# Routed experts: the inner rows are turned by a transposing DMA instead of by TensorE

## The reference, cut to what matters

```
h   = (x @ W1[e]) * silu(x @ W3[e])        # 256 -> 512 inner features
y   = h @ W2[e]                            # 512 -> 256
out = sum over the two experts of gate * y
```

## Time and profile before

| | us |
|---|---|
| median of 3 runs | 1129.15 (1126.81 to 1134.13) |
| the profiled execution, its own time | 1125.32 |
| its span | 1123.5 |
| mean granted TensorE clock, share of full speed | 0.967 |
| PE busy over the span | 1001.6 (89%) |
| POOL busy over the span | 568.2 (51%) |

### The profile page before, as it was taken

How to read it: one execution, slowest core, us unless ns; L and a number is a source line. 1 busy time by engine, 2 the same in 40 slices (tenths; PEclk the granted TensorE clock), 3 DMA queues, 4 the chain that set the end, 5 groups by cost and what they waited for, 6 DMA issues and landing times. The chain is left out here.

```text
span 1123.5 us, 27288 instructions
## 1 busy us (share of the span) xinstructions
PE 1001.6 (89%) x9398; PEld 770.3 (69%) x9398; DVE 745.6 (66%) x1732; ACT 547.1 (49%) x1091; POOL 568.2 (51%) x743
## 2 busy tenths in 40 slices
PE   5898888677699899999999999949998995999998
PEld 3666666455488756666666666627787884898987
DVE  6999999756376634444544445558999974666663
ACT  5888888632255433333332222334443434766764
POOL 6776767205354479999991293047656501000000
PEclk9999999978699999999999999979999998999999
DMA  4454444347599684554221111323443312111110
GB/s 140 149 160 150 143 152 130 98 143 223 184 310 323 216 247 154 170 174 160 86 62 48 48 53 53 99 80 104 127 131 114 109 38 66 39 58 38 56 48 29
DMA packets 113819, 137.96 MB, mean 123 GB/s; under 512 B 12352, under 2 KB 102432, under 8 KB 111904
## 3 DMA queue, kind: packets, MB, share of 16 engines
q1 hardware_dynamic: 104464, 101.63, 29.0%
q0 software_dynamic: 9232, 34.67, 9.3%
HBM read 83.96 MB, written 52.30 MB: 121 GB/s over the span
## 5 line engine op out<-in xcount | busy, mean ns | idle before, releaser
L1121 ACT CAST hT<-HT 128x512 f16<-128x512 f32 x71 | 41.7, 587 | 184.5 <-PE HT L1063 184.5
L943 POOL DMA_INDIRECT xs_d<-ht,slot x64 | 67.2, 1050 | 85.8 <-DMA ht<-h_d 39.3
L1070 PE MATMUL Ye<-wm,hT 128*128 x852 | 105.1, 273 | 1.7 <-DVE hT L1155 1.5
L1070 PE MATMUL Ge<-wm,xT 128*128 x426 | 104.8, 383 | 1.0 <-DVE xT L1159 1.0
L1070 PE MATMUL Ue<-wm,xT 128*128 x426 | 103.7, 379 | 0.0
L1070 PEld LDWEIGHTS Ye<-wm,hT 128*128 128x128 f16 x852 | 83.0, 98 | 25.8 <-issue 3.1
L1866 ACT ACTIVATE gf<-H,bup,wdesc 128x256 f32<-128x256 f32 x128 | 72.1, 565 | 50.0 <-DVE g L1835 32.8
L1894 PE MATMUL H<-T6s,wm 128*128 128x256 f16 x768 | 95.5, 275 | 0.9 <-DVE T6s L1830 0.9
L1906 PE MATMUL Y<-wm,g 128*128 128x256 f16 x768 | 93.8, 273 | 1.6 <-DVE g L1835 1.6
L1835 DVE SCALAR_TENSOR_TENSOR g<-gf,g 128x512 f16<-128x512 f32 x64 | 44.5, 695 | 67.8 <-ACT g L1871 67.7
L1360 POOL DMA_INDIRECT yg<-ys_d,slot x64 | 64.6, 1009 | 39.1 <-POOLq L1009 21.8
(11 more groups left out here) (273 smaller groups left out, 2523.3 us busy)
## 6 DMA issues: line engine op xcount, KB each, us to landing
stage<-in_L_ffn_W_dram SPq DMA_DIRECT2D x24, 512.0 KB
xs_d<-zeros SPq DMA_DIRECT2D x36, 256.0 KB, 2.6
ys_d<-ye SPq DMA_DIRECT2D x71, 128.0 KB, 1.7
xe<-xs_d SPq DMA_DIRECT2D x69, 128.0 KB, 2.3
bw<-in_L_ffn_up_weights_dram POOLq DMA_DIRECT2D x7, 1024.0 KB, 6.6
bw<-_L_ffn_down_weights_dram POOLq DMA_DIRECT2D x7, 1024.0 KB, 5.3
xb<-in_x_dram SPq DMA_DIRECT2D x32, 128.0 KB, 2.4
cb<-in_ctx_dram SPq DMA_DIRECT2D x32, 128.0 KB, 2.3
```

Of the source, the lines that this page charges most:

```text
L943: nc.gpsimd.indirect_dma_start(out=xs_d[:, :], out_offset=bass.IndirectOffsetOnAxis(ap=slot[:, j, 2 * t + i:2 * t + i + 1], axis=0), in_=h ...
L1070: last = nc.tensor.matmul(bank, left[:, xp, c, :], wm[:, kind, bass.ds(e, 1), wp, c * width:(c + 1) * width], start=i == 0 and c == 0, sto ...
```

## The change

The LO and HI halves of the inner rows are now made before they are turned, as rows: ACT casts `he` to `hs[HI]`, and DVE subtracts, `hs[LO] = he - hs[HI]`. Both inputs of that subtraction are SBUF tensors; before, one was the PSUM tile `HT`. Then one DMA a tile, `dma_start_transpose`, issued by SP, turns all 128x1024 float16 elements of `hs` and writes `hT` (256 KB). PE's four transposes a tile, and the PSUM tile `HT`, go. The down product of tile t is now made in tile t + 2's place instead of tile t + 1's, so the loop has one more round, and `hT` has three buffers instead of two.

```diff
-            hT = sb("hT", [P, 2, 2, HC, P], F16)
+            hs = sb("hs", [P, 2, 2, H], F16)
+            hT = sb("hT", [P, 3, 2, HC, P], F16)
...
-            HT = ph.enter_context(nc.psum_tensor("HT", [P, HC, P], F32))
...
SP
-                    for t in range(-2, NE + 1):
+                    for t in range(-2, NE + 2):
...
-                        if t >= 1:
-                            sp.wait_ge(s_yc, t)
-                            sp.dma_start(ys_d[(t - 1) * P:t * P, :], ye[:, (t - 1) % 2, :]).then_inc(s_yst[(t - 1) % 2], 16)
+                        if 0 <= t < NE:
+                            sp.wait_ge(s_hl4, BASE_L + t + 1)
+                            if t >= 3:
+                                sp.wait_ge(s_ye, t - 2)
+                            sp.dma_start_transpose(hT[:, t % 3, :, :, :].rearrange("p l c n -> p (l c) n"),
+                                                   hs[:, t % 2, :, :].rearrange("p l n -> p (l n)")).then_inc(s_hT[t % 2], 16)
+                        if t >= 2:
+                            sp.wait_ge(s_yc, t - 1)
+                            sp.dma_start(ys_d[(t - 2) * P:(t - 1) * P, :], ye[:, t % 2, :]).then_inc(s_yst[t % 2], 16)
PE
-                    def inner_rows(t):
-                        if t >= 0:
-                            pe.wait_ge(s_he, t + 1)
-                            if t >= 1:
-                                pe.wait_ge(s_hTe, t)
-                            for c in range(HC):
-                                last = nc.tensor.transpose(HT[:, c, :], he[:, t % 2, c * P:(c + 1) * P], ident[:, :])
-                            last.then_inc(s_hT, 1)
...
-                        if t >= 1:
-                            pe.wait_ge(s_hTe, t)
-                            if t >= 3:
-                                pe.wait_ge(s_yc, t - 2)
-                            product(Ye[(t - 1) % 2][:, :], hT[:, (t - 1) % 2, :, :, :], 2, before, HC, D).then_inc(s_ye, 1)
+                        if t >= 2:
+                            pe.wait_ge(s_hT[t % 2], 16 * (t // 2))
+                            if t >= 4:
+                                pe.wait_ge(s_yc, t - 3)
+                            product(Ye[t % 2][:, :], hT[:, (t - 2) % 3, :, :, :], 2, experts.pop(t - 2), HC, D).then_inc(s_ye, 1)
ACT
-                            act.wait_ge(s_hT, t)
+                            act.wait_ge(s_he, t)
                             if t >= 3:
-                                act.wait_ge(s_ye, t - 2)
-                            nc.scalar.copy(hT[:, (t - 1) % 2, HI, :, :], HT[:, :, :]).then_inc(s_hh4, 1)
+                                act.wait_ge(s_hT[(t - 1) % 2], 16 * ((t - 1) // 2))
+                            nc.scalar.copy(hs[:, (t - 1) % 2, HI, :], he[:, (t - 1) % 2, :]).then_inc(s_hh4, 1)
DVE
                             dve.wait_ge(s_hh4, t)
-                            nc.vector.tensor_tensor(hT[:, (t - 1) % 2, LO, :, :], HT[:, :, :], hT[:, (t - 1) % 2, HI, :, :],
-                                                    ALU.subtract).then_inc(s_hTe, 1)
+                            nc.vector.tensor_tensor(hs[:, (t - 1) % 2, LO, :], he[:, (t - 1) % 2, :], hs[:, (t - 1) % 2, HI, :],
+                                                    ALU.subtract).then_inc(s_hl4, 1)
```

More of the change, by code:

```diff
@@ L999, in build_program @@
             s_xt, s_xte, s_g, s_u, s_sl4, s_he = (sem(n) for n in ("s_xt", "s_xte", "s_g", "s_u", "s_sl4", "s_he"))
-            s_hT, s_hTe, s_ye, s_yc = (sem(n) for n in ("s_hT", "s_hTe", "s_ye", "s_yc"))
+            s_hT = sems("s_hT", 2)
+            s_ye, s_yc = sem("s_ye"), sem("s_yc")
+            s_hl4, BASE_L = s_ot, NB
             s_yst = sems("s_yst", 2)
@@ L1086, in _ @@
                     input_rows(0)
[L1087 to L1090, removed]
+                    experts = {}
+                    for t in range(NE + 2):
                         if t < NE:
+                            e = experts[t] = pe.value_load(tile_expert[0:1, t:t + 1], min_val=0, max_val=E - 1)
                             pe.wait_ge(s_xte, t + 1)
@@ L1106, in _ @@
                                 fold(t - MID - 1)
-                        if t >= 1:
-                            pe.wait_ge(s_hTe, t)
-                            if t >= 3:
-                                pe.wait_ge(s_yc, t - 2)
-                            product(Ye[(t - 1) % 2][:, :], hT[:, (t - 1) % 2, :, :, :], 2, before, HC, D).then_inc(s_ye, 1)
-                        before = e
+                        if t >= 2:
[3 more added lines that the diff above has]
+                            product(Ye[t % 2][:, :], hT[:, (t - 2) % 3, :, :, :], 2, experts.pop(t - 2), HC, D).then_inc(s_ye, 1)
                 @block.scalar
@@ L1150, in largest @@
                                                 apply_absolute_value=True).then_inc(s_bv, 1)
-                    for t in range(-1, NE + 1):
-                        if t >= 1:
+                    for t in range(-1, NE + 2):
+                        if 1 <= t <= NE:
                             dve.wait_ge(s_hh4, t)
-                            nc.vector.tensor_tensor(hT[:, (t - 1) % 2, LO, :, :], HT[:, :, :], hT[:, (t - 1) % 2, HI, :, :],
-                                                    ALU.subtract).then_inc(s_hTe, 1)
+                            nc.vector.tensor_tensor(hs[:, (t - 1) % 2, LO, :], he[:, (t - 1) % 2, :], hs[:, (t - 1) % 2, HI, :],
+                                                    ALU.subtract).then_inc(s_hl4, 1)
                         if t + 1 < NE:
@@ L1164, in _ @@
                             if t >= 2:
-                                dve.wait_ge(s_hT, t - 1)
+                                dve.wait_ge(s_hh4, t - 1)
                             STT(he[:, t % 2, :], Ue[t % 2][:, :], ES / (XS * WS), sg4[:, t % 2, :],
@@ L1171, in _ @@
                             folded(t - MID - 1)
[L1172 to L1176, removed]
+                        if t >= 2:
+                            dve.wait_ge(s_ye, t - 1)
+                            if t >= 4:
+                                dve.wait_ge(s_yst[t % 2], 16 * (t // 2 - 1))
+                            nc.vector.tensor_scalar(ye[:, t % 2, :], Ye[t % 2][:, :], 1 / (ES * WS), None,
                                                     ALU.mult).then_inc(s_yc, 1)
```

## The result

| | before | after |
|---|---|---|
| median of the runs, us | 1128.45 (4 runs) | 1154.30 (4 runs, 1148.01 to 1164.43) |
| ratio to before, 95% interval | | 1.0231 [1.0169, 1.0293] |
| profiled execution, us (span) | 1125.32 (1123.5) | 1148.01 (1146.3) |

The changed kernel is 2.3% slower.

The account below looks back on a forecast made before the run. PE was taken to set the pace, with POOL's chain bounding the meeting at tile 43. +24.8 - 11.9 + 1.6 + 2.8 = +17.3 us on the profiled 1125.3 gave 1142.6, as run median 1146, range 1118 to 1158.

Parts of the forecast that it names:

- The meeting point: At tile 43 PE waits for POOL's chain, whose end was to move from 595.3 to about 620.1 us.
- the exclusion of DVE and POOL: Beside POOL's chain, a DVE operation with two SBUF inputs and a POOL operation exclude each other; the later stands still.
- PE's pace: In the routed experts, a tile falls from 4.55 to 4.11 us once PE's 0.44 us transpose group goes.
- it waits for at most one POOL instruction: Beside POOL's chain, DVE's subtraction waits for at most one POOL instruction, some 1.55 us a tile, harmless to DVE.
- POOL loses 0.62 us a tile, 24.8 in all: Before tile 43, subtractions hit POOL's chain 40 times at 0.62 us each, lengthening it by 24.8 us.
- The first rival: Before tile 43, POOL is not slowed by the subtractions; the change gives -7.5 us, 1122 in all; chance 0.20.
- The transposing DMA: 3.6 us and hidden: In each tile the DMA lands in 3.6 us of 5.6 available, so PE does not wait for it.
- The second rival: In every tile the DMA lands later than a tile allows, 1257 or 1523 us in all; chance 0.13.
- After the meeting, -11.9 us: Past tile 43, 27 transpose groups go before the last tile's up product, saving 11.9 us.
- the tail: From the last tile's up product to the last down product's end: 7.9 us instead of 5.1, +2.8.
- The cold clock after one long stand, +1.6: After PE's long stand at tile 43, its first products run at a lower clock, costing 1.6 us.
- POOL's second chain 52.0 us, hidden: After the first chain, POOL's second grows by 6.8 to 52.0 us, thinly hidden before DVE asks for it.

Follow-up runs that it names:

- experiments 1 and 2: 1: changed kernel with `he` in PSUM, 1133.27 us. 2: kernel before plus an unused two-SBUF-input DVE subtraction a tile, 1188.42 us.
- experiment 3: Changed kernel with POOL waiting for its own semaphore after each multiplication, not only after the fourth: 1148.63 us, ratio 1.0191 to the kernel before.
- experiment 4: Changed kernel with POOL's eleven first loads issued one behind each of its chain's first eleven steps: 1147.18 us, ratio 1.0178 to the kernel before.

## Why the prediction was right, step by step

The forecast was 1146 (1118 to 1158); measured were 1154.3 and, in the profiled execution that the sum was made for, 1148.0 against 1142.6. The meeting point was to move by 24.6 us and moved by 28.2. That the time would be lost before the meeting, and that the exclusion of DVE and POOL would be at work in it, was right. Who waits for whom was not, and that the size is near is luck: with the 11.0 us that POOL really lost in place of 24.8 the forecast's sum is +3.5 us, not +17.3. Waits that it had put at nothing made up the rest, 26.8 us for the DMA and 7.3 for `xT`.

- *PE's pace.* Right. The tile is 4.12 us (608.41 to 612.53) for 4.11, where PE waits for nothing.
- *DVE's subtraction and POOL's operations exclude each other.* Right, by experiments 1 and 2. Undisturbed it takes 0.68.
- *"For DVE this is harmless: it waits for at most one POOL instruction."* This is the step that failed. It waited for up to four in a row, 6.74 us. The timeline held one POOL instruction at a time, and from them "the later one stands still" was carried over to a row of four issued without a wait between them. "One instruction" holds in fourteen of the chain's 26 steps, and in experiment 3, where POOL pauses after each; in the other twelve it does not.
- *The Trainium skill's rule* in "SBUF — State Buffer", "Who interferes with whom", that the second to issue is blocked until the first has finished, describes experiment 3 and the fourteen steps. In the twelve others of the changed kernel the blocked side stayed out for up to four instructions.
- *POOL loses 0.62 us a tile, 24.8 in all.* Mis-sized. The chain is 195.6 us for 184.55: 11.0, or 0.26 a tile over 42 tiles. POOL loses 0.34 where a subtraction gets in at a pause and some 0.45 where it gets in inside a row; 29 POOL operations were held so, and the other subtractions ran while POOL had no arithmetic in hand. The first rival had half of this ("DVE might get in only where POOL pauses, and POOL lose almost nothing"), and it had put PE at the meeting at about 602 with DVE starved by 3 us a tile. By its own figures, 2.2 + 3 us a tile for 4.11, forty times, that should have read about 619. PE came at 623.7, but not for that reason alone: that rival, too, took the DMA for free.
- *The transposing DMA: 3.6 us and hidden; on SP "nothing".* Right in a quiet stretch: 3.1 us in the median, beside 3.8 for a plain 256 KB load of the same run. There the trace agrees with the Trainium skill's "Advanced Engine Details and Errata", "X-Bar Transpose (TRN2)" (as fast as plain ones); the 10.5 us that the prediction worked out from the Trainium skill's "VectorE: DVE Perf Modes" is not seen. Wrong beside bulk loads: issue 9.03 and landing 14.7 at worst, 26.8 us of PE's waits before the meeting. The second rival priced a DMA that is slow always, not one that is slow in company, and the share of the DMA engines, 0.50 before, was not in the argument at all.
- *After the meeting, -11.9 us.* From `fold_bias` to the end came -4.7, where -11.9 + 2.8 for the tail = -9.1 was expected. Two tiles with waits for the DMA (1.17 and 1.41) behind SP's loads for the next stage took 3.9 us more than their neighbours, and the sixteen tiles with a fold each became 0.34 us shorter (4.92 for 5.25), not 0.44, another 1.5. The tail itself cost 7.35 - 5.1 = 2.2 for 2.8.
- *The cold clock after one long stand, +1.6.* That stand did not occur. The shorter ones, of up to 11.19 us, were followed by four slow products, 4.9 us in all.
- *POOL's second chain 52.0 us, hidden.* Right: 49.6, nobody waits.
- *"What would show it"* served its purpose: PE standing 40 to 50 us for POOL was to be seen, and is not in the trace. Of its other signs, POOL's longest multiplication (2.27 us for 2.2) came true. On the time alone the forecast would have passed as understood.

## What to carry to other kernels

Where a DVE operation with two SBUF inputs is put beside a busy POOL, look for rows of POOL instructions without a wait between them, and price DVE's wait once by one instruction and once by the whole row: here both occurred, in steps of different operand form. One input from PSUM removed the wait. Before work is moved to DMA, read the DMA share of the stretch as one reads an engine's busy share: at 0.50 there was not room for a transpose of 256 KB in each tile beside POOL's 1 MB blocks, and the price came as rare, long waits and as spread between runs. When PE, POOL and DMA all run within a few us of each other, curing one delay shows the next: with `he` in PSUM, or with later loads besides, the kernel was no faster than before; with the third tile of distance it was, by 0.6% without the later loads and 0.9 to 1.7% with them.

## What the runs showed of the hardware that was not expected

- A DVE subtraction with two SBUF inputs (0.68 us) stayed out through four back-to-back POOL multiplications, 6.74 us; up to 8.11 us in experiment 4. With one input in PSUM its longest was 0.69. With a semaphore wait after each multiplication it was 2.49.
- That happened in twelve steps of the chain and never in the other fourteen, where it got in between two POOL instructions with no wait between them (1.14 us at 584.06). What makes the difference is open.
- When it got in at a pause, POOL's next instruction took 0.34 us longer, half the subtraction's length; inside a row, 0.45.
- The issue of a 256 KB transposing DMA holds SP's queue 1.24 us in the median, and it took 9 to 15 us at worst beside POOL's loads. The other DMAs of that queue stand behind it.
- With the transposing DMA the DMA engines' share rose from 0.50 to 0.89 for 170 and 212 GB/s: it costs more of their time than its bytes say. 75,000 more packets were moved in the run (188,795 for 113,819).
